# Cross attentions: projections one per three steps, output projection and division in steps of their own, norms over four steps

## The chip, the cores and the metric

The kernel runs on one core of one Trainium2 chip. A core has TensorE (PE, with its weight loads as PEld), VectorE (DVE), ScalarE (ACT), GpSimd (POOL) and SyncE (SP), which here issues the transfers. Each engine works through its own list of instructions in order; semaphores tie the lists together. The metric is the device time of one execution in microseconds, lower is better.

## What is computed

Six layers of a decoder, each followed by a residual and a layer norm, on an input of 32 batches x 128 tokens x 128 features. Two of them, `cross0` and `cross1`, are the cross attentions that the change touches; they differ in that the first adds a mask. Cut to what matters:

```python
q = heads(tgt @ Wq + bq) / sqrt(8)        # 16 heads of 8 features
k = heads(memory @ Wk + bk)
v = heads(memory @ Wv + bv)
scores = einsum('bhqd,bhkd->bhqk', q, k)
scores = where(mask[:, None, :, :], NEG_INF, scores)     # first cross attention only
attn = softmax(scores, axis=-1)
ctx = einsum('bhqk,bhkd->bhqd', attn, v).transpose(0, 2, 1, 3).reshape(b, -1, 128)
x = layernorm(x + ctx @ Wo + bo)
```

The other four passes (self attention, two mixtures of experts, attention over positions) are the same in both kernels.

## The kernel before

`cross_attention_pass` holds each cross attention. A batch is a row `r` (32 of them, in 8 quads `q` of four), and a row is split into four units `u` of four heads each, 128 units in all. The loop `for s in steps` runs on every engine over the same step numbers, one unit per step, and `at(s, lag, per, count)` says which item, if any, is due in a step: item `i` comes in step `lag + per * i`. So the lags and the order of the `if` blocks inside a step set each engine's order. A quad is 16 steps, a row four. In what follows a step is odd or even by its number, counted within a row as 0 to 3.

The work of a unit, in the order of the data:

- `scores` (L990; in the masked pass after two mask matmuls, L984): query rows x keys, for two units at a time, in odd steps. VectorE takes the maxima (L1188), POOL splits them into two bf16 parts (L1137, L1139), PE transposes them (`maxT`, L1047) and ScalarE copies them back (L1109).
- `scoresT`: the transposed scores of unit s+2 (L1034, in the masked pass after the mask matmul L1001), interleaved with the subtraction of the maxima of unit s+1 (L1037). Each unit of the 32-row products sits in one of four groups of 32 rows of the array, and the two interleaved ones in different groups, as do the two units of `scores`.
- ScalarE takes the exponential twice, as f16 and as f32 (L1103, L1104), POOL subtracts the one from the other (L1131, `pl`).
- `attended` (L953 to L955 on `avp`): 12 matmuls with 9 columns each, for unit s-2, at the end of the step. It fills one PSUM tile over four steps; VectorE takes the reciprocal (L1176), then a maximum, then the division (`att`, L1194) in the step with number 2 of the row.
- Per row: PE transposes `att` (`attT`, L1058, step 3), ScalarE and VectorE split it (L1113, L1199), PE multiplies with the output weights (L953 to L955 on `msc`, in step 1), VectorE adds the residual (L1225) and takes the statistics (L1232, L1181).
- Per quad: five pieces in `prep` (transposed x, Q, transposed context, K, V), one PSUM tile `prj` for all. Before, one is due every two steps, K twelve and V ten steps ahead of the quad's first unit. SP then lays Q and K out into the four row groups with 12 copies each (L903), loads the next quads (L886, L890, L895) and stores a finished quad (L936). The norm of a quad (L1238, four instructions) stands in one step.

`maxT`, `attT` and the output projection share one PSUM tile, `msc`. `take_misc` makes each wait until the previous user has been read. In the step with number 1 PE runs scoresT, scores, `maxT`, output projection, attended; the output projection waits there for ScalarE's copy of the maxima (`s_mTs`).

## Time and profile before

| | us |
|---|---|
| median of 3 runs | 2220.37 |
| lowest and highest | 2205.09, 2227.87 |
| profiled execution, its own time | 2225.0 |
| its span | 2223.2 |
| PE, DVE, ACT, POOL busy | 1489.2, 1237.8, 793.8, 1011.7 |
| first cross attention, from first to last transfer | 765 to 1174 |
| second cross attention | 1673 to 2000 |

Busy times are sums over passes with different limits, so the page's totals don't say what a step of one pass waits for. For that the stretches of one quad and the lists of waits are read. Weight loads and matmuls overlap, matmul ends are modelled, and a few records of matmuls are missing (of the mask matmul L1001, 66 of 128 are there). PEclk is the share of the full clock that TensorE was granted: 1.0 is 2.4 GHz, 0.5 is 1.2 GHz.

### The profile page before, as it was taken

How to read it: one execution, taken by the hardware profiler on the slowest of the kernel's cores; microseconds unless marked ns; L12 is line 12 of the kernel's file. 1: busy time of each engine (PE TensorE's matmuls, PEld its weight loads, DVE VectorE, ACT ScalarE, POOL GpSimd, SP SyncE). 2: the span in 40 equal slices, each digit the busy share in tenths (PEclk: the TensorE clock that was granted, in tenths of full speed). 3: DMA queues.
4: the chain of work that ended last, by engine and by line, in shares of the span. 5: the costliest groups of instructions: out<-in, count | busy, mean ns of one | idle time of the engine just before them, and what ended most of it. 6: DMA issues, size and time to landing. Idle time of an engine off the chain costs nothing. (4 is left out here: it accounts for less than half of the span.)

```text
span 2223.2 us, 45449 instructions
## 1 busy us (share of the span) xinstructions
PE 1489.2 (67%) x17246; PEld 1022.1 (46%) x17428; DVE 1237.8 (56%) x2931; ACT 793.8 (36%) x1668; POOL 1011.7 (46%) x1132
## 2 busy tenths in 40 slices
PE   4799999999999668888873118890043677753180
PEld 1466656666666434444443107780042455543170
DVE  4688888788896334444436314453462555554354
ACT  2344444444444224444441103330032565541330
POOL 4656455374471225455554650006613566561506
PEclk9999999999999655555655558995585555555595
DMA  2000000000000111111105211222222111104422
GB/s 88 1 9 10 4 10 4 10 9 5 10 4 5 28 39 42 32 33 36 43 6 172 87 46 51 61 65 56 65 71 59 50 37 52 41 19 142 151 70 71
DMA packets 141816, 99.76 MB, mean 45 GB/s; under 512 B 21283, under 2 KB 129101, under 8 KB 141476
## 3 DMA queue, kind: packets, MB, share of 16 engines
q1 hardware_dynamic: 135460, 84.64, 12.8%
q0 software_dynamic: 6144, 12.22, 1.8%
q8 instruction: 143, 2.34, 0.4%
q14 instruction: 69, 0.57, 0.1%
HBM read 50.99 MB, written 33.55 MB: 38 GB/s over the span
## 5 line engine op out<-in xcount | busy, mean ns | idle before, releaser
L1131 POOL TENSOR_TENSOR cross_pl<-cross_pf,cross_ph 128x512 f16<-128x512 f32 x256 | 292.9, 1157 | 156.9 <-ACT cross_pf L1104 137.4
L639 POOL TENSOR_TENSOR own_full<-own_rot 128x512 f32<-128x512 f32 x128 | 162.7, 1271 | 159.3 <-DVE own_rot L714 149.7
L1624 POOL DMA_INDIRECT mix_got<-results,mix_fetch x96 | 95.6, 996 | 284.1 <-DMA results<-mix_yo 256.8
L1188 DVE TENSOR_REDUCE cross_negmax<-cross_scores 128x8 f32<-128x1024 f32 x128 | 152.5, 1191 | 78.0 <-PE cross_scores L990 77.8
L1103 ACT ACTIVATE cross_ph<-cross_scoresT 128x512 f16<-128x512 f32 x256 | 154.9, 605 | 48.1 <-PE cross_scoresT L1037 43.4
L1034 PE MATMUL cross_scoresT<-cross_qt,cross_kt 32*128 32x128 f16 x1024 | 152.0, 299 | 26.2 <-issue 21.8
L631 POOL TENSOR_TENSOR own_qkl<-own_full,own_qkh 128x512 f16<-128x512 f32 x128 | 157.8, 1236 | 0.0
L1104 ACT ACTIVATE cross_pf<-cross_scoresT 128x512 f32<-128x512 f32 x256 | 155.7, 608 | 0.0
L1037 PE MATMUL cross_scoresT<-cross_maxT,cross_sel 32*128 32x128 bf16 x1024 | 152.2, 299 | 0.0
L553 ACT CAST own_qkh<-own_full 128x512 f16<-128x512 f32 x128 | 79.1, 618 | 158.6 <-POOL own_full L639 156.6
L575 ACT ACTIVATE own_ph<-own_scoresT 128x512 f16<-128x512 f32 x128 | 76.5, 598 | 153.1 <-PE own_scoresT L491 153.1
L265 DVE TENSOR_TENSOR own_pl<-own_pf,own_ph 128x512 f16<-128x512 f32 x128 | 127.1, 993 | 1.0 <-ACT own_pf L576 1.0
L953 PE MATMUL cross_attended<-cross_vl,cross_ph 128*128 128x9 f16 x1024 | 114.3, 178 | 19.6 <-DVE cross_att L1194 17.8
L953 PEld LDWEIGHTS cross_attended<-cross_vl,cross_ph 128*128 128x128 f16 x1024 | 103.0, 114 | 46.2 <-DVE cross_att L1194 30.2
L1176 DVE RECIPROCAL cross_recip<-cross_attended 128x16 f32<-128x16 f32 x64 | 16.5, 257 | 186.0 <-PE cross_attended L955 186.0
L1789 DVE SCALAR_TENSOR_TENSOR mix_hl<-mix_pH,mix_hh 128x512 f16<-128x512 f32 x112 | 72.1, 685 | 85.5 <-ACT mix_hh L1569 85.5
L484 PE MATMUL own_scoresT<-own_qkh,own_qkl 64*128 64x128 f16 x512 | 113.6, 222 | 7.3 <-issue 2.1
L1034 PEld LDWEIGHTS cross_scoresT<-cross_qt,cross_kt 32*128 32x128 f16 x1024 | 85.6, 124 | 64.3 <-issue 55.8
L491 PE MATMUL own_scoresT<-own_maxT,own_sel 64*128 64x128 bf16 x512 | 112.7, 220 | 0.0
L486 PE MATMUL own_scoresT<-own_qkh 64*128 64x128 f16 x512 | 112.6, 220 | 0.0
L485 PE MATMUL own_scoresT<-own_qkl,own_qkh 64*128 64x128 f16 x512 | 112.4, 220 | 0.0
L954 PE MATMUL cross_attended<-cross_vh,cross_pl 128*128 128x9 f16 x1024 | 105.0, 169 | 0.0
(332 smaller groups left out, 5451.1 us busy)
## 6 DMA issues: line engine op xcount, KB each, us to landing
mix_stage<-in_mix_w SPq DMA_DIRECT2D x48, 256.0 KB
slots<-mix_blank SPq DMA_DIRECT2D x14, 512.0 KB, 5.9
mix_xg<-slots SPq DMA_DIRECT2D x56, 128.0 KB
results<-mix_yo SPq DMA_DIRECT2D x56, 128.0 KB, 1.8
cross_xin<-after SPq DMA_DIRECT2D x16, 256.0 KB, 2.9
cross_cin<-in_ctx SPq DMA_DIRECT2D x16, 256.0 KB, 3.3
cross_qt<-cross_qnh SPq DMA_DIRECT2D x128, 32.0 KB
cross_kt<-cross_knh SPq DMA_DIRECT2D x128, 32.0 KB
```

The lines of the kernel that those rows point to most:

```text
L265: ops.tensor_tensor(pl[g][:], pf[g % 2][:], ph[g][:], ALU.subtract).then_inc(s_plow, 1)
L484: nc.tensor.matmul(o, kl_, qa, start=False, stop=False, skip_group_check=True)
L491: mm = nc.tensor.matmul(o, sel[r:r + nr, g // 2 if own else g, j, :], maxT[bb % 2][r:r + nr, :], start=False, stop=True, skip_group_check= ...
L631: nc.gpsimd.tensor_tensor(qkl[1 - par][p % 2][:, p // 2, :], full[p % 2][:], qkh[1 - par][p % 2][:, p // 2, :], ALU.subtract)\
L639: nc.gpsimd.tensor_tensor(full[g % 2][:], rot[g % 2][0][:], rot[g % 2][1][:], ALU.add)\
L953: nc.tensor.matmul(out, lh, rl, start=start, stop=False, skip_group_check=True)
L1034: nc.tensor.matmul(out, lhs, rhs, start=first, stop=False, skip_group_check=True)
L1037: mm = nc.tensor.matmul(out, lhs, rhs, start=False, stop=True, skip_group_check=True)
L1103: nc.scalar.activation(ph[u % 4][:], stp[u % 3][:], ACT.Exp, scale=scale)
L1104: nc.scalar.activation(pf[u % 3][:], stp[u % 3][:], ACT.Exp, scale=scale).then_inc(s_exp, 1)
L1131: nc.gpsimd.tensor_tensor(pl[u % 4][:], pf[u % 3][:], ph[u % 4][:], ALU.subtract).then_inc(s_pl, 1)
L1188: nc.vector.tensor_reduce(negmax[rr % 2][:, 2 * a:2 * a + 2, :].rearrange("p u g -> p (u g)"), scp[:].rearrange("p (h t) -> p h t", t=P), ...
```

## The change

Only `cross_attention_pass` changes. The computation and the instructions are the same; their order and their waits are not.

- `prep`: the five pieces of a quad are due at -25, -22, -19, -16, -13 instead of -18, -16, -14, -12, -10. VectorE takes them two steps later instead of one; SP's layouts move to -18 and -14, the loads to -34.
- PE: within a step attended now follows scoresT at once, then `maxT`, `attT`, the scores, the pieces, the output projection. The output projection moves from lag 9 to 10, to the end of step 2.
- ScalarE: the copies of the maxima and of `attT` stand ahead of the exponentials, the pieces behind them.
- VectorE: the division directly follows the reciprocal, ahead of the maximum; residual and statistics come one step later each; the norm's four instructions stand in four different odd steps (27, 29, 31, 33).
- POOL: rstd in step 26 instead of 23. SP: store in step 34 instead of 25.
- `ident4` is loaded with the first constants, so PE, ACT and DVE wait for 48 of `s_const` and 64 of `s_more`.

```diff
-        FIRST, LAST = -18, NU + 26
+        FIRST, LAST = -25, NU + 18
...
-            return [(p, i) for p, lag in ((XT, -18), (Q, -16), (CT, -14), (K, -12), (V, -10))
+            return [(p, i) for p, lag in ((XT, -25), (Q, -22), (CT, -19), (K, -16), (V, -13))
...
-                q = at(s, -15, 16, NQUAD)
+                q = at(s, -18, 16, NQUAD)
                 if q is not None:
                     lay(q, Q, qt, (qnh, qnh, qnl))
-                q = at(s, -11, 16, NQUAD)
+                q = at(s, -14, 16, NQUAD)
                 if q is not None:
                     lay(q, K, kt, (knh, knl, knh))
-                q = at(s, -24, 16, NQUAD)
+                q = at(s, -34, 16, NQUAD)
                 if q:
                     load_x(q)
...
-                r = at(s, 9, UNITS, B)
-                if r is not None:
-                    pe.wait_ge(s_al, r + 1)
-                    take_misc((s_y, r + 1))
-                    three(msc[:, 0:D], attTh[:], attTl[:], wh["o"][:], wl["o"][:], True, True).then_inc(s_o, 1)
...
+                pair = at(s, -7, 2, NU // 2)
+                if pair is not None:
+                    scores(pair)
+                for p, q in prep(s):
+                    project(p, q)
+                r = at(s, 10, UNITS, B)
+                if r is not None:
+                    pe.wait_ge(s_al, r + 1)
+                    take_misc((s_y, r + 1))
+                    three(msc[:, 0:D], attTh[:], attTl[:], wh["o"][:], wl["o"][:], True, True).then_inc(s_o, 1)
...
-                q = at(s, 23, 16, NQUAD)
+                q = at(s, 26, 16, NQUAD)
...
+                    dve.wait_ge(s_rec, r + 1)
+                    late(dve, s_aT, r - 1)
+                    nc.vector.tensor_tensor(att[r % 2][:], v[:, :, 0:DH], recip[:].unsqueeze(2).to_broadcast([P, H, DH]),
+                                            ALU.mult).then_inc(s_att, 1)
...
+                for b in range(QUAD):
+                    q = at(s, 27 + 2 * b, 16, NQUAD)
...
-                for p, q in prep(s - 1):
+                for p, q in prep(s - 2):
```

How the order changes. The first place is PE in the second cross attention, the step in which the maxima are transposed (L990 is the scores, L1047 `maxT`, L953 to L955 on `cross_misc` the output projection, on `cross_attended` attended). Before:

```order
L1034 MATMUL cross_scoresT<-cross_qt,cross_kt 128x128
L1037 MATMUL cross_scoresT<-cross_maxT,cross_sel 128x128
L990 MATMUL cross_scores<-cross_kt,cross_qt 128x128 x8
L1047 MATMUL cross_misc<-cross_ident,cross_max 128x128
L953 MATMUL cross_misc<-cross_wol,cross_attTh 128x128
L954 MATMUL cross_misc<-cross_woh,cross_attTl 128x128
L955 MATMUL cross_misc<-cross_woh,cross_attTh 128x128
L953 MATMUL cross_attended<-cross_vl,cross_ph 128x9
```

The scores directly follow scoresT, and the output projection directly follows `maxT`. The same step after the change (one line further down in the file: L991 is the scores, L1060 `maxT`, L964 a transposed input piece, L1035 and L1038 the next step's scoresT):

```order
L954 MATMUL cross_attended<-cross_vl,cross_ph 128x9
L955 MATMUL cross_attended<-cross_vh,cross_pl 128x9
L956 MATMUL cross_attended<-cross_vh,cross_ph 128x9
L1060 MATMUL cross_misc<-cross_ident,cross_max 128x128
L991 MATMUL cross_scores<-cross_kt,cross_qt 128x128 x8
L964 MATMUL cross_proj<-cross_ident,cross_cin 128x128 x4
L1035 MATMUL cross_scoresT<-cross_qt,cross_kt 128x128
L1038 MATMUL cross_scoresT<-cross_maxT,cross_sel 128x128
```

Attended has moved between scoresT and the scores, and the output projection has left the step: it now ends the next one.

The second place is ScalarE, one row's worth of exponentials up to the copy of the maxima (L1113 copies `attT`, L1109 the maxima). Before:

```order
L1113 CAST cross_attTh<-cross_misc 128x128
L1103 ACTIVATE cross_ph<-cross_scoresT 128x512
L1104 ACTIVATE cross_pf<-cross_scoresT 128x512
L1103 ACTIVATE cross_ph<-cross_scoresT 128x512
L1104 ACTIVATE cross_pf<-cross_scoresT 128x512
L1103 ACTIVATE cross_ph<-cross_scoresT 128x512
L1104 ACTIVATE cross_pf<-cross_scoresT 128x512
L1109 COPY cross_maxT<-cross_misc 128x128
```

And after (L1094 copies `attT`, L1090 the maxima, L1105 takes a piece):

```order
L1094 CAST cross_attTh<-cross_misc 128x128
L1100 ACTIVATE cross_ph<-cross_scoresT 128x512
L1101 ACTIVATE cross_pf<-cross_scoresT 128x512
L1105 CAST cross_xh<-cross_proj 128x512
L1100 ACTIVATE cross_ph<-cross_scoresT 128x512
L1101 ACTIVATE cross_pf<-cross_scoresT 128x512
L1090 COPY cross_maxT<-cross_misc 128x128
L1100 ACTIVATE cross_ph<-cross_scoresT 128x512
```

The copy now stands behind two exponential pairs instead of three.

The third place is the queue of SP in the masked pass, the layouts of one quad (`qt`, `kt`) and the loads of the next. Before:

```order
L903 DMA cross_qt<-cross_qnh 8x4x512 x8
L903 DMA cross_qt<-cross_qnl 8x4x512 x4
L903 DMA cross_kt<-cross_knh 8x4x512 x4
L903 DMA cross_kt<-cross_knl 8x4x512 x4
L903 DMA cross_kt<-cross_knh 8x4x512 x4
L886 DMA cross_xin<-after 128x4x128
L890 DMA cross_cin<-in_ctx 128x4x128
L895 DMA cross_rawmask<-in_mask 128x4x128
```

And after:

```order
L903 DMA cross_qt<-cross_qnh 8x4x512 x8
L903 DMA cross_qt<-cross_qnl 8x4x512 x4
L886 DMA cross_xin<-after 128x4x128
L890 DMA cross_cin<-in_ctx 128x4x128
L895 DMA cross_rawmask<-in_mask 128x4x128
L903 DMA cross_kt<-cross_knh 8x4x512 x4
L903 DMA cross_kt<-cross_knl 8x4x512 x4
L903 DMA cross_kt<-cross_knh 8x4x512 x4
```

The loads have moved from behind K's layout to the place between Q's and K's.

## Rows read from the trace of the kernel before

**Rows 1.** The page's slices: granted clock in tenths, 40 slices of 55.6 us

```profile
PEclk9999999999999655555655558995585555555595
```

**Rows 2.** Busy time in stretches, first cross pass: one quad, then a fast stretch

```profile
core 0: us, PE busy (x) PEld busy (x) DVE busy (x) ACT busy (x) POOL busy (x), PEclk, DMA share, GB/s
...
904.45:950.63 46.18, 40.76 (x455) 22.64 (x462) 19.65 (x41) 21.51 (x46) 23.86 (x28) 0.50 0.13 38
1056.00:1066.00 10.00, 6.78 (x125) 4.27 (x123) 6.60 (x13) 5.33 (x12) 6.84 (x10) 1.00 0.22 66
```

**Rows 3.** Busy time in stretches, same columns: one quad of the second cross pass

```profile
1788.47:1824.05 35.58, 25.91 (x430) 18.57 (x430) 20.21 (x41) 20.61 (x46) 22.19 (x27) 0.50 0.15 46
```

**Rows 4.** Waits 780 to 1180 us: waiting and waited for, us in total, times, longest

```profile
PE cross_scores L984 <- DMA cross_kt<-cross_knh: 17.3, 4, 11.2
...
PE cross_misc L953 <- ACT cross_maxT L1109: 13.7, 29, 1.2
...
PE cross_attended L953 <- DVE cross_att L1194: 7.0, 12, 0.6
```

**Rows 5.** Waits 1690 to 2000 us, the second cross pass

```profile
PE cross_misc L953 <- ACT cross_maxT L1109: 38.9, 29, 1.9
...
PE cross_scores L990 <- DMA cross_kt<-cross_knh: 34.5, 8, 11.8
...
PE cross_attended L953 <- DVE cross_att L1194: 10.8, 10, 1.1
```

**Rows 6.** Timeline of PE: start, duration, engine, line, operation, idle before and releaser

```profile
800.85 1.03 PE L984 MATMUL cross_scores<-cross_addmask,cross_ident 128*128 128x512 bf16 x2 [1.32 <-DVE cross_negmax L1188]
```

**Rows 7.** Timeline of the second cross pass: ScalarE's copy, then PE

```profile
1825.05 0.30 ACT L1109 COPY cross_maxT<-cross_misc 128x128 bf16<-128x128 bf16 x1
1825.49 0.26 PE L953 MATMUL cross_misc<-cross_wol,cross_attTh 128*128 128x128 f16 x1 [1.89 <-ACT cross_maxT L1109]
...
1828.31 0.28 PE L1034 MATMUL cross_scoresT<-cross_qt,cross_kt 32*128 32x128 f16 x1
...
1828.34 0.29 PE L990 MATMUL cross_scores<-cross_kt,cross_qt 32*128 32x128 f16 x2
...
1828.87 0.47 PE L1058 MATMUL cross_misc<-cross_ident,cross_att 128*128 128x128 f32 x1
...
1829.59 0.28 PE L1034 MATMUL cross_scoresT<-cross_qt,cross_kt 32*128 32x128 f16 x1
...
1830.12 0.61 PE L953 MATMUL cross_proj<-cross_cl,cross_wkh 128*128 128x512 f16 x1
```

**Rows 8.** Timeline of PE, first cross pass: masks that begin a step

```profile
840.15 0.59 PE L1001 MATMUL cross_scoresT<-cross_ident,cross_addmask 128*128 128x512 bf16 x1
...
844.75 0.59 PE L1001 MATMUL cross_scoresT<-cross_ident,cross_addmask 128*128 128x512 bf16 x1
...
1104.04 0.38 PE L1001 MATMUL cross_scoresT<-cross_ident,cross_addmask 128*128 128x512 bf16 x1
...
1107.22 0.39 PE L1001 MATMUL cross_scoresT<-cross_ident,cross_addmask 128*128 128x512 bf16 x1
1110.15 0.69 PE L984 MATMUL cross_scores<-cross_addmask,cross_ident 128*128 128x512 bf16 x2 [2.22 <-DMA cross_kt<-cross_knh]
```

**Rows 9.** Timeline of SP's queue: two loads, the last layout group of a quad

```profile
796.32 0.44 SPq L886 DMA_DIRECT2D cross_xin<-after  x1
...
797.36 0.51 SPq L895 DMA_DIRECT2D cross_rawmask<-in_mask  x1
...
1105.67 2.81 SPq L903 DMA_DIRECT2D cross_kt<-cross_knh  x4
```

**Rows 10.** Timeline of DVE and POOL: maximum and second half of the split

```profile
899.87 1.22 DVE L1188 TENSOR_REDUCE cross_negmax<-cross_scores 128x8 f32<-128x1024 f32 x1 [1.07 <-PE cross_scores L990]
...
901.44 0.22 POOL L1139 TENSOR_TENSOR cross_max<-cross_negmax,cross_max 128x16 bf16<-128x16 f32 x1
```

**Rows 11.** Timeline of PE: low-clock scores, K projection before a rise, scores after

```profile
842.18 0.61 PE L990 MATMUL cross_scores<-cross_kt,cross_qt 32*128 32x128 f16 x8
...
1096.96 0.61 PE L953 MATMUL cross_proj<-cross_cl,cross_wkh 128*128 128x512 f16 x1
...
1100.48 0.40 PE L990 MATMUL cross_scores<-cross_kt,cross_qt 32*128 32x128 f16 x8
```

More of the change, by code:

```diff
@@ L908, in _ @@
             sp.dma_start(bias[:], w["bias"]).then_inc(s_const, 16)
+            sp.dma_start(ident4[:], k["ident4"]).then_inc(s_const, 16)
             for n in names[0:2]:
@@ L913, in _ @@
                 sp.dma_start(stage[n][:], w[n]).then_inc(s_w[n], 16)
-            for to, frm in ((ident4[:], k["ident4"]), (sel[:], k["sel"]), (vbias[:], w["vbias"]), (expo[:], k["expo4"]),
+            for to, frm in ((sel[:], k["sel"]), (vbias[:], w["vbias"]), (expo[:], k["expo4"]),
                             (obias[:], w["obias"].partition_broadcast(P))):
@@ L1082, in _ @@
                 nc.scalar.copy(wh[n][:], stage[n][:]).then_inc(s_wh, 1)
-            act.wait_ge(s_const, 32)
+            act.wait_ge(s_const, 48)
             for s in steps:
+                r = at(s, -2, UNITS, B)
+                if r is not None:
+                    act.wait_ge(s_mT, r + 1)
+                    late(act, s_T, UNITS * (r - 1))
+                    nc.scalar.copy(maxT[r % 2][:], msc[:, 0:P // 2].bitcast(BF16)).then_inc(s_mTs, 1)
+                r = at(s, 8, UNITS, B)
+                if r is not None:
+                    act.wait_ge(s_aT, r + 1)
+                    nc.scalar.copy(attTh[:], msc[:, 0:P]).then_inc(s_ah, 1)
+                u = at(s, 0, 1, NU)
+                if u is not None:
+                    act.wait_ge(s_T, u + 1)
+                    late(act, s_av, u - 3)
+                    late(act, s_pl, u - 2)
+                    nc.scalar.activation(ph[u % 4][:], stp[u % 3][:], ACT.Exp, scale=scale)
+                    nc.scalar.activation(pf[u % 3][:], stp[u % 3][:], ACT.Exp, scale=scale).then_inc(s_exp, 1)
                 for p, q in prep(s - 1):
@@ L1166, in _ @@
                 if i == 1:
-                    dve.wait_ge(s_const, 32)
-                    dve.wait_ge(s_more, 16 * 5)
+                    dve.wait_ge(s_const, 48)
+                    dve.wait_ge(s_more, 16 * 4)
                     nc.vector.tensor_copy(vbias_b[:], vbias[:].to_broadcast([P, P])).then_inc(s_vb, 1)
```

122 lines of the change are left out of this document (48 added, 74 removed).

## Prediction

> **What bounds the kernel now.** I read first the slices of the page: the two cross attentions (765 to 1174 us and 1672 to 2000 us) stand in the slices where the granted clock is 5 and not 9 [rows 1]. So TensorE runs there at 1.2 GHz, and the first question is how much of it is work and how much is waiting. A stretch of exactly one quad (16 steps, four batches) tells it. In the first pass a quad takes 46.18 us, with PE busy for 40.76 [rows 2]; the mask matmul of L1001 (0.59 us [rows 8]) is recorded in only about half of the steps, and the eight missing ones, about 0.4 us each beside their neighbours, make PE some 44 us busy. In the second pass a quad takes 35.58 us with PE busy for 25.91, and the next engine, POOL, for 22.19 [rows 3]. The first cross pass is therefore bound by PE at the low clock, the second by waits of PE. The list of waits names them. In the first pass PE waited 13.7 us for ScalarE's copy of the transposed maxima, 7.0 for VectorE's division, and 17.3 for the K transfers, of which 11.2 is one wait at the start [rows 4]. In the second pass the same three are 38.9, 10.8 and 34.5, of which 11.8 at the start [rows 5]. A fourth, 1.32 us for VectorE's maximum, comes twice at the start of each pass [rows 6].
>
> Why the maxima's copy is so late shows in the timeline: ScalarE copies at 1825.05, behind the exponentials of two units, and PE, which asks for the output projection in the same step as that transposition, starts it at 1825.49 after 1.89 us idle [rows 7].
>
> **The change, term by term.** *Output projection one step later, copy ahead of the exponentials.* Between the transposition and the output projection now lie the scores (odd step) and the next step's scoresT and attended; the copy is ScalarE's first work of its step. The wait goes: 13.7 + 38.9 us. Cover if I am wrong: 0.45 us per row (32 rows a pass), the smallest value now.
>
> *Attended ahead of the scores, division straight after the reciprocal.* Before, the division stands behind a 1.2 us maximum while PE is already at the next row's attended. Now attended ends ahead of `maxT` and the scores, earlier by their length, and nothing stands between reciprocal and division: 7.0 + 10.8 us go.
>
> *Projections earlier.* K is projected nine steps before its first scores instead of five. The queue then needs 24 copies of 0.70 us (groups of four in 2.81 us) and two or three loads of 0.5 between Q and K [rows 9]; the last copy landed about 1.7 us after its issue, if the start of the scores at 1110.15 is set against the last group's start at 1105.67 [rows 8, 9]. That is 16.9 + 1.5 + 1.7 = 20 us, counted from the scoresT that frees the Q buffer, eleven steps ahead of the scores. A second-pass quad of work alone is 25.9 us busy now [rows 3] and 8 x 0.5 us for the scores (below), 29.9 in all; eleven steps of it are 20.6, and the place in the step adds 1. So the wait goes, by a small margin in the second pass and a wide one in the first: 22.7 + 6.1 us. Also the second quad's transposes and Q now fill the ramp, where PE waits for VectorE: 2 x 2 x 1.32 = 5.3 us.
>
> Together 29.4 us in the first pass (13.7 + 7.0 + 6.1 + 2.6) and 75.0 in the second: 104. I take 100, since the last rows of a pass have no later work to cover them.
>
> *What it adds.* The scores lose their company. In the second pass scoresT and the eight scores matmuls now run side by side: from 1828.31 to 1828.87, 0.56 us for both, while a step without scores needs 0.53 (1829.59 to 1830.12) [rows 7]. After the change attended, which uses all rows of the array, stands between them. Eight scores matmuls alone lie between 0 (if they overlap the next scoresT) and their 0.54 us; the next scoresT needs one of the same two row groups, so I take 0.5: 64 x 0.5 = 32 us (0 to 35). In the first pass the mask matmuls separated them already: 0. The Trainium skill, TensorEngine Tiling (Array Packing), Key Properties, says that different tiles of the array load and multiply in parallel and that a change of tiling mode drains the engine. The rows agree with the first half, and it is the rule that speaks against this change; if the scores kept a partner the sum would be 32 us lower.
>
> The loads of the second quad now stand ahead of K in the queue at the start: 796.32 to 797.87 for three [rows 9], so 1.5 and 1.0 us later first scores. Norms in four pieces, earlier rstd, ident4 in another group: the same instructions; VectorE and POOL have 20 and 22 us of work in 35.6 [rows 3], which hides them; uncovered, 0.1 us each.
>
> Sum with the clock as now: 100 - 32 - 2.5 = 65 us. The profiled execution took 2225 us (span 2223.2), 5 more than the median 2220: 2225 - 65 = 2160.
>
> **The clock.** The first pass is not at the low clock throughout. At 1056 to 1066 it was granted 1.00 [rows 2]. The matmuls show it too: between two masks, the same two steps took 4.60 us (840.15 to 844.75) at 1.2 GHz and 3.18 (1104.04 to 1107.22) at 2.4 [rows 8]. Before it rose, PE had run a K projection, scoresT and the scores' masks with one short attended among them (1096.96 on; the scores at 1100.48 take 0.40 us for the eight, at the low clock 0.61) [rows 11]. It fell back each time when PE stood idle for the K transfers, 2.2 us at 1110.15 [rows 8]. The change works on both ends: scores, V projection, mask and scoresT now follow each other with no attended (9 narrow columns per weight load) between, once a quad, and the idle time that ended the fast stretches goes. I expect the rise in the first or second quad and then mostly the high clock: six of eight quads. A quad without waits is 46.2 - 2.4 = 43.8 us at the low clock; times 1.42/4.60 it gains 13.5. Six give 81. The three fast stretches that are in the 2225 already were worth about 7 us, which go off: 2160 + 7 - 81 = **2086 us**. POOL's 23.86 us a quad [rows 2] stays below the 30 that result. The second pass has no masks and so less dense stretches; it stays low.
>
> **Rivals.** *The clock behaves as before* (0.28): the dense stretch doesn't suffice, or, with steps of 1.6 to 1.7 us, K comes late again (20 us against eleven steps of 1.7 = 19) and PE's idle time takes the clock down each quad. For it: only three rises in the whole pass now. 2160, 2140 to 2185.
> *Both passes at the high clock* (0.06). The second pass then falls from 29.9 us a quad toward POOL's 22.2; with the queue's 20 us for eleven steps and POOL's 1.1 to 1.4 for each of five it is about 25.5: 7.5 quads x 4.4 = 33 us less, 2053. Against it: not one fast slice in the second pass now. The Trainium skill, TensorE: Matmul & The Clock Gate, section on why this matters for kernels, advises to avoid idle gaps between bursts to keep the full clock. The trace doesn't agree with that alone: a quad with under 3 us idle in 46 ran at 0.50 [rows 2]; by the page this rival would be the likeliest.
> *The waits move* (0.07): half of the 100 comes back as waits for exponentials or divisions: 2225 - 50 + 34 = 2209, no change.
> *The other side, slower* (0.05): the split of the maxima. The scores are now last in their step, and PE asks for maxT two steps on, after two scoresT and two attended: 0.53 + 0.45 twice = 1.96 us in the second pass. The chain in between is the maximum and two POOL operations, from 899.87 to 901.66, 1.8 us [rows 10]. It fits with 0.15 to spare. If the 1.16 us subtraction on POOL or a norm and a projection piece on VectorE (0.6 + 0.7) come first, PE waits up to 2 us in each of 64 rows: 2160 + 128 = 2288. It decides from 1.0 us per row, which eats the 65. Against it: the subtraction in front belongs to a unit whose exponential ended a step earlier.
>
> **Numbers.** My forecast has 0.54 (own range 2055 to 2130: four to eight fast quads). A difference under 1% (22 us) can't be told from none here. Faster: 0.54 + 0.28 + 0.06 = 0.88; same 0.07; slower 0.05. The range 2045 to 2185 holds the first three cases to their bounds.
>
> **What would show it.** PE's waits for the maxima's copy and the division gone from both passes; a second-pass quad near 29.9 us with PE nearly without idle time; scores alone 0.5 us between transposition and next scoresT; the K wait only at the start; the granted clock above 0.8 over the first pass. A clock of 0.5 there makes it 2160; a wait at the maxT transposition for POOL is the slower case; a clock of 1.0 in the second pass shows that I underrated the density.

## The result and the profile after

| | before | after |
|---|---|---|
| median of 3 runs | 2220.37 | 2093.04 |
| lowest and highest | 2205.09, 2227.87 | 2071.41, 2097.38 |
| profiled execution, its span | 2223.2 | 2091.2 |

The ratio is 0.941, with a 95% interval of 0.928 to 0.954: faster by 5.9%. The two spans differ by 132.0 us. To see where they went, each execution is cut where a pass's first transfer is issued (SP's load at L886 for a cross attention, the mixture's or the position attention's first one behind it). These cuts give the table; "high" is the time within the first cross attention at a granted clock of 1.0, summed from the trace's record of that clock, from its first scores on.

| us | self attention and start | first cross | high | second cross | the three other passes together |
|---|---|---|---|---|---|
| before | 765.2 | 408.8 | 23.9 | 326.7 | 722.5 |
| after | 748.4 | 340.5 | 95.6 | 280.0 | 722.3 |
| difference | -16.8 | -68.3 | | -46.7 | -0.2 |

The page of the changed kernel gives the same picture in two lines: PE's busy tenths, and the granted clock, in slices of 52.3 us. The first cross attention is slices 15 to 21, the second slices 31 to 36.

```profile
PE   4799999999999939999964218891052899953370
...
PEclk9999999999999955569855559996575555555695
```

Where [rows 1] had nothing above 6 in the first cross attention, there are now a 6, a 9 and an 8; the second stays at 5 (slice 31, a 6, begins in the pass before it).

The waits of PE in the first cross attention (748 to 1089 us), then in the second (1587 to 1868 us): waiting and waited for, us in total, times, longest. They answer to [rows 4, 5].

```profile
PE cross_scores L985 <- DMA cross_kt<-cross_knh: 11.4, 3, 7.5
...
PE cross_attended L954 <- POOL cross_pl L1132: 3.0, 5, 0.6
PE cross_misc L1060 <- POOL cross_max L1140: 1.9, 1, 1.9
...
PE cross_scores L991 <- DMA cross_kt<-cross_knh: 13.5, 8, 7.9
...
PE cross_attended L954 <- POOL cross_pl L1132: 3.7, 7, 0.9
PE cross_misc L1060 <- POOL cross_max L1140: 2.1, 2, 1.9
...
PE cross_attended L954 <- DVE cross_att L1180: 1.1, 3, 0.4
```

The wait for ScalarE's copy of the maxima is gone from both lists, the division's from the first and nearly from the second. K's is not only at the start (7.5 and 7.9 us): in the second pass 5.7 us are left in the seven later quads. A stretch of one quad in each pass, in the columns of [rows 2], answers to [rows 2, 3]:

```profile
831.07:874.05 42.98, 42.98 (x463) 21.81 (x464) 19.30 (x39) 21.80 (x46) 23.60 (x29) 0.50 0.11 34
...
1715.45:1744.92 29.47, 28.57 (x435) 19.59 (x434) 20.88 (x42) 21.30 (x47) 22.11 (x28) 0.50 0.18 56
```

The first-pass quad at the low clock takes 43.0 us with PE busy throughout; the second-pass quad takes 29.5 with PE busy for 28.6, where before it was busy for 25.9 of 35.6.

### The profile page after: what moved, and what is told of

Same layout as the page of the kernel before. It is cut to its first block and busy times, and to the rows that moved or that the text cites. A ratio compares the mean times of both kernels' runs of the same rounds, so it can differ in the third digit from the quotient of the medians.

```text
span 2091.2 us, 45631 instructions
## 1 busy us (share of the span) xinstructions
PE 1488.2 (71%) x17428; PEld 1001.5 (48%) x17428; DVE 1248.5 (60%) x2931; ACT 800.6 (38%) x1668; POOL 1008.7 (48%) x1132
## 5 line engine op out<-in xcount | busy, mean ns | idle before, releaser
L1035 PE MATMUL cross_scoresT<-cross_qt,cross_kt 32*128 32x128 f16 x1024 | 143.2, 285 | 0.1
L1038 PE MATMUL cross_scoresT<-cross_maxT,cross_sel 32*128 32x128 bf16 x1024 | 142.4, 281 | 0.0
L1035 PEld LDWEIGHTS cross_scoresT<-cross_qt,cross_kt 32*128 32x128 f16 x1024 | 85.3, 121 | 69.8 <-issue 58.8
L954 PE MATMUL cross_attended<-cross_vl,cross_ph 128*128 128x9 f16 x1024 | 108.7, 173 | 8.1 <-POOL cross_pl L1132 6.7
L954 PEld LDWEIGHTS cross_attended<-cross_vl,cross_ph 128*128 128x128 f16 x1024 | 86.4, 102 | 53.5 <-issue 38.6
L714 DVE SCALAR_TENSOR_TENSOR own_rot<-own_proj,own_bias,own_cos 128x512 f32<-128x512 f32 x128 | 94.9, 742 | 17.2 <-POOL own_full L639 12.8
L956 PE MATMUL cross_attended<-cross_vh,cross_ph 128*128 128x9 f16 x1024 | 104.2, 168 | 0.0
```

The lines of the kernel that those rows point to most:

```text
L954: nc.tensor.matmul(out, lh, rl, start=start, stop=False, skip_group_check=True)
L1035: nc.tensor.matmul(out, lhs, rhs, start=first, stop=False, skip_group_check=True)
L1038: mm = nc.tensor.matmul(out, lhs, rhs, start=False, stop=True, skip_group_check=True)
```

## The experiments

All lengths below are those of the two cross attentions, cut as above, from one profiled execution each. Medians are of whole executions; a ratio is to the kernel before on the same chip and occasion, whose median there lay between 2212.6 and 2224.7. The diffs are cut to their main lines; the recorded text behind each says what else moved.

| kernel | first cross | high | second cross | median | ratio to before, 95% |
|---|---|---|---|---|---|
| before | 408.8 | 23.9 | 326.7 | 2220.4 | |
| 1. before + projections early | 414.8 | 17.1 | 320.2 | 2219.9 | 0.998 (0.994 to 1.002) |
| 2. before + output projection's own step | 383.8 | 51.2 | 316.4 | 2181.2 | 0.983 (0.977 to 0.989) |
| 3. before + attended and division | 399.1 | 51.2 | 327.8 | 2211.2 | 0.994 (0.990 to 0.999) |
| 8. after, old projections | 373.3 | 92.2 | 310.0 | 2172.3 | 0.979 (0.976 to 0.983) |
| after | 340.5 | 95.6 | 280.0 | 2093.0 | 0.941 (0.928 to 0.954) |
| 12. after, once more | 344.6 | 85.3 | 281.2 | 2103.8 | 0.943 (0.937 to 0.949) |
| 11. after, norm in one step | 325.6 | 129.7 | 285.0 | 2109.6 | 0.953 (0.949 to 0.958) |
| 4. after, scores behind scoresT | 321.3 | 160.4 | 276.4 | 2076.8 | 0.936 (0.931 to 0.941) |
| 7. as 4, loads behind K | 343.1 | 150.2 | 294.3 | 2127.0 | 0.957 (0.952 to 0.962) |
| 5. after, three buffers | 312.8 | 146.8 | 276.3 | 2077.8 | 0.937 (0.933 to 0.941) |
| 6. as 4, three buffers | 281.9 | 211.6 | 265.1 | 2038.0 | 0.921 (0.915 to 0.927) |
| 9. as 6, pieces two steps earlier | 282.2 | 218.5 | 263.3 | 2033.8 | 0.917 (0.912 to 0.922) |
| 10. as 9, extra product in second pass | 285.6 | 211.6 | 269.9 | 2036.1 | 0.919 (0.913 to 0.925) |

### One part at a time

**1. Projections early, the rest as before.**

```diff
-            return [(p, i) for p, lag in ((XT, -18), (Q, -16), (CT, -14), (K, -12), (V, -10))
+            return [(p, i) for p, lag in ((XT, -25), (Q, -22), (CT, -19), (K, -16), (V, -13))
...
-                q = at(s, -15, 16, NQUAD)
+                q = at(s, -18, 16, NQUAD)
...
-                q = at(s, -11, 16, NQUAD)
+                q = at(s, -14, 16, NQUAD)
```

> The kernel before with one part of the change: the five pieces of a quad at -25 to -13 (VectorE two steps behind), Q's layout at -18, K's at -14, loads at -34. ScalarE's pieces stand behind its copies, since else two engines would wait for each other. Lengths are from a pass's first transfer to the next pass's; before they are 408.8 us (first cross attention) and 326.7 (second). Theory A, the waits add up as the prediction has them: the K wait from the second quad on goes, 22.7 us in the second pass and 6.1 in the first, and the ramp 2.6 each, less 1.5 and 1.0 for the loads: second pass 303 us, first 402, clock as before. Rival B, the spacing is what lets the clock rise in the first pass: first pass near 340. Rival C, PE waits elsewhere instead (for the exponentials, behind which the pieces no longer stand, or for the maxima's copy): second pass 320 or more.

Median 2219.9, the same as before; first cross attention 414.8 us, second 320.2. Waits of PE in seven quads of the second pass, of the kernel before (1717 to 1966 us), then of this one (1717 to 1965 us):

```profile
PE cross_misc L953 <- ACT cross_maxT L1109: 35.3, 26, 1.9
PE cross_scores L990 <- DMA cross_kt<-cross_knh: 22.7, 7, 6.9
PE cross_attended L953 <- DVE cross_att L1194: 8.7, 8, 1.1
```

```profile
PE cross_misc L954 <- ACT cross_maxT L1097: 32.8, 27, 1.4
PE cross_attended L954 <- DVE cross_att L1195: 30.7, 26, 1.5
PE cross_scores L991 <- DMA cross_kt<-cross_knh: 4.7, 1, 4.7
```

The K wait fell from 22.7 us to 4.7, all of it in one quad, and the division's rose from 8.7 to 30.7. A quad stays at 35.4 us. This is rival C: the time went into another wait. Part of it may lie in ScalarE's pieces, which stand behind the exponentials here; that was not taken apart. The first pass had no more of the high clock than before (17.1 us against 23.9), so the spacing of the projections alone doesn't raise it (rival B falls).

**2. Output projection in its own step, ScalarE's copies ahead of the exponentials.**

```diff
-                r = at(s, 9, UNITS, B)
-                if r is not None:
-                    pe.wait_ge(s_al, r + 1)
...
+                r = at(s, 10, UNITS, B)
+                if r is not None:
+                    pe.wait_ge(s_al, r + 1)
...
             for s in steps:
+                r = at(s, -2, UNITS, B)
+                if r is not None:
+                    act.wait_ge(s_mT, r + 1)
```

> The kernel before with one part: output projection one step later, ScalarE's copies of the maxima and of attT ahead of the exponentials, and what follows on VectorE and POOL moved with it; attended, division and projections as before. Theory A: the wait for the maxima's copy goes, 38.9 us in the second pass and 13.7 in the first; but the K transfers still have only eight to nine steps, and each of them is now 0.3 us shorter in the second pass, so the K wait grows by up to 2.6 us a quad, 18 in all. Second pass 326.7 - 38.9 + 18 = 306 us (288 if K keeps up), first pass 408.8 - 13.7 = 395, clock as before. Rival B: the idle time between steps is what keeps the clock low in the first pass: then it rises here too, first pass 340 to 360. Rival C: the wait moves to attT or the output projection itself: second pass 320 or more.

Median 2181.2; first cross attention 383.8, second 316.4. The wait for the copy is gone, and K's takes much of it back (second pass, 1680 to 1924 us):

```profile
PE cross_scores L990 <- DMA cross_kt<-cross_knh: 36.5, 7, 6.6
PE cross_attended L953 <- DVE cross_att L1194: 18.6, 14, 3.0
```

K 22.7 to 36.5, the division 8.7 to 18.6. Theory A had the direction and K's part (up to 18), but not the division's, so it gave 306. The first pass is 25 us shorter with 27 us more at the high clock: some of rival B, in one profile.

**3. Attended behind scoresT, division behind the reciprocal.**

```diff
+                    dve.wait_ge(s_rec, r + 1)
+                    late(dve, s_aT, r - 1)
+                    nc.vector.tensor_tensor(att[r % 2][:], v[:, :, 0:DH], recip[:].unsqueeze(2).to_broadcast([P, H, DH]),
+                                            ALU.mult).then_inc(s_att, 1)
                 pair = at(s, -6, 2, NU // 2)
```

> The kernel before with one part: attended directly behind scoresT, the division directly behind the reciprocal. Theory A: the division's wait goes (10.8 us second pass, 7.0 first), and the scores lose their company in the second pass: 64 x 0.42 to 0.5 = +27 to 32 us, of which the K wait, which has eight to nine of sixteen steps, takes back about half: second pass 326.7 - 10.8 + 29 - 9 = 336 us; first pass 402 with the clock as before. Rival B: the maxima's copy comes less late since PE asks for it later in the step, so second pass 326 or less. Rival C: the order without attended between scores, V, mask and scoresT is what raises the clock in the first pass: first pass 340 to 370.

Median 2211.2; first cross attention 399.1, second 327.8. Neither 336 nor below 326: the waits left in the second pass (1700 to 1950 us) are

```profile
PE cross_misc L953 <- ACT cross_maxT L1109: 21.4, 26, 1.3
PE cross_scores L990 <- DMA cross_kt<-cross_knh: 13.4, 7, 4.9
```

so the maxima's copy fell from 35.3 to 21.4 us, which theory A left out, and K's from 22.7 to 13.4, as it had it; PE's extra work filled the rest. The first pass came out near theory A's 402, and not at rival C's 340 to 370: its clock rises in five quads, each time behind a K projection and the next mask, and each time for 10.2 us only, up to a K wait of some 1.7 us.

**8. The changed kernel with the old projections.**

```diff
-            return [(p, i) for p, lag in ((XT, -25), (Q, -22), (CT, -19), (K, -16), (V, -13))
+            return [(p, i) for p, lag in ((XT, -18), (Q, -16), (CT, -14), (K, -12), (V, -10))
```

> The changed kernel with the pieces, layouts and loads at their old lags (-18, -16, -14, -12, -10; -15, -11; -24), all else changed. It tells whether the parts add up. Theory A, they don't: each wait covers the next, and with K projected nine steps... that is five steps ahead of its scores the K chain sets the quad at about 34.8 us whatever PE saves elsewhere, as it did where only the output projection was moved: second pass 312 to 318 us, K waits of 35 or more. Rival B, the parts add up, so only the early K's 22.7 us are missing: 303 us. First pass at the low clock: K has time there, so 384 to 400 us, and if the early projections are not needed for the clock to rise, 340 to 360.

Second cross attention 310.0 us, a little below theory A's range (a quad of 33.3 to 34.3), with the K waits that it gave (1680 to 1917 us):

```profile
PE cross_scores L991 <- DMA cross_kt<-cross_knh: 37.1, 7, 6.5
```

The first took 373.3 us, between both ranges given for it, with 92.2 us at the high clock. So the early projections aren't needed for the clock to rise. In the second pass the three parts alone are worth 6.5, 10.3 and -1.1 us, 15.7 together; all at once 46.7, of which some 5 are the norm's (kernel 11), which none of the three has. Early projections alone brought 6.5 us, as the last part 30.0. **The parts don't add up: the waits of one quad lie over each other**, and as long as K takes some twenty microseconds from a late start, whatever PE saves elsewhere it spends waiting there.

### What bounds the second cross attention now

**4. Scores directly behind scoresT again.**

```diff
                 if u1 is not None:
                     mm.then_inc(s_T, 1)
+                pair = at(s, -7, 2, NU // 2)
+                if pair is not None:
+                    scores(pair)
...
-                pair = at(s, -7, 2, NU // 2)
-                if pair is not None:
-                    scores(pair)
```

> The changed kernel with one part undone: the scores directly behind scoresT again, attended behind them. Changed kernel: 340.5 us in the first cross attention, 280.0 in the second. Theory A: the overlap comes back in the second pass, 64 x 0.42 = 27 us less work, but eleven steps are then 18 us against a K chain of 19 to 20, so 1 to 2 us a quad of K wait come back: 263 us (253 to 266). In the first pass the scores follow scoresT and attended stands ahead of V projection and mask again: if the row without attended is what raised the clock, the pass goes back to 390 us; rival B, it was the missing idle time, the pass stays at 330 to 350. Rival C, attended, now last ahead of the maxima's transposition, is late for VectorE's division, which costs 0.5 us a row: second pass 275 or more.

**5. Three buffers for the laid-out Q and K.**

```diff
-        qt, kt = many(2, "qt", [P, HU, WIDTH], F16), many(2, "kt", [P, HU, WIDTH], F16)
+        qt, kt = many(3, "qt", [P, HU, WIDTH], F16), many(3, "kt", [P, HU, WIDTH], F16)
...
-                late(sp, s_T, 4 * UNITS * (q - 1))
+                late(sp, s_T, 4 * UNITS * (q - 2))
```

> The changed kernel with three buffers for the laid-out Q and K instead of two (zeroed by two more memsets), Q's layout asked for at -20. The queue then needn't wait for the previous quad's last scoresT. Changed kernel: 340.5 and 280.0 us, PE busy 28.6 us of a second-pass quad of 29.2. Theory A: with the scores last in their step the second pass is bound by PE itself, since the scores lost their company: only the 5.7 us of K waits go, 274 us. Rival B, the K chain is what sets the 29.2 us quad and PE's busy time is stretched to it: 262 us or less. First pass: the K waits of the fast quads go, 3.9 us, and if it is the idle time at K that takes the clock down, the fast stretches become longer: 340 - 4 to 340 - 20 us.

**6. Both edits, 4's and 5's, together** (the two diffs above).

> The changed kernel with the scores directly behind scoresT and with three buffers for Q and K: the previous run's edit and the one of the scores together. With the scores first and two buffers the second pass took 276.4 us, with 21.6 us of K waits in seven quads, PE busy 25.9 us of a quad of 29.1. Theory A: the K chain was the bound there, and the overlap of the scores was worth 27 us but hidden behind it: second pass 276.4 - 21.6 = 255 us, a quad of 26.2. Rival B: PE waits for exponentials or for POOL instead (POOL is busy 22.4 us of a quad): 265 us or more. First pass: 321.3 us with two buffers, of which 10.3 is K waits from the second quad on: 311 us if the clock stays as it is, 295 to 305 if these waits are what takes it down.

The second pass took 276.4 us with kernel 4, 276.3 with 5 and 265.1 with 6. One quad of each, 4, 5 and 6 in turn, in the columns of [rows 2]:

```profile
1662.12:1691.81 29.69, 25.66 (x435) 17.42 (x434) 20.50 (x42) 20.89 (x46) 22.26 (x28) 0.50 0.19 55
```

```profile
1685.60:1714.30 28.70, 28.51 (x436) 19.59 (x433) 21.42 (x43) 21.20 (x46) 22.13 (x28) 0.50 0.20 58
```

```profile
1658.58:1685.95 27.37, 25.39 (x423) 17.13 (x421) 20.49 (x43) 20.59 (x45) 22.22 (x28) 0.50 0.20 61
```

These are two limits of nearly the same size. With the scores last PE is busy for 28.5 us of 28.7 (kernel 5): PE is the bound, and the scores' lost company is 28.57 - 25.66 = 2.9 us a quad, 0.36 for each of eight scores. With the scores first (kernel 4) PE needs only 25.7, but its quads take 29.0 to 29.7, because K is late; its waits in seven quads (1604 to 1808 us) are

```profile
PE cross_scores L991 <- DMA cross_kt<-cross_knh: 21.6, 7, 4.5
PE cross_scoresT L1035 <- ACT cross_pf L1101: 3.9, 10, 0.4
```

Either edit alone is worth 4 us in the second pass, both together 15: again more than their sum. For kernel 4 rival C's length came (276.4 against "275 or more"), but not by its cause, the division, which costs 0.2 us there: theory A had the cause, and undersized the K wait (3.1 us a quad, not 1 to 2). Kernel 6 missed its 255 by 10 us: the K wait is still 10.2 us in seven quads, since with the third buffer Q's layout starts as soon as the low half of Q is there, which in turn is late (SP waited 56.1 us for it in those quads). The first passes took 312.8 us (expected 320 to 336) and 281.9 (295 to 311), with 146.8 and 211.6 us at the high clock. For kernel 4 I had expected 390 us there if the row without attended counts, since attended now stood ahead of the V projection; it came out at 321.3, 9 us below rival B's 330 to 350; the section on the clock comes back to it.

**7. As kernel 4, with the loads behind K's layout.**

```diff
-                q = at(s, -34, 16, NQUAD)
+                q = at(s, -29, 16, NQUAD)
```

> The changed kernel with the scores directly behind scoresT, two buffers, and the next quads' loads asked for behind K's layout (-29) instead of between Q's and K's (-34). Theory A: if a second-pass quad is the K chain (24 copies of 0.70, the landing, and the two loads between) plus the six steps outside it, then it gets 1.0 us shorter by the two loads: 276.4 - 7.5 x 1.0 = 269 us, and in the first pass 1.5 us a quad at the high clock: 321 - 10 = 311. Rival B, the loads cost the queue nothing because the copies wait for something else (their data): 276 as before.

A miss: 294.3 us instead of 269. The wait moved from K to the next quad's input (second pass, 1657 to 1882 us):

```profile
PE cross_proj L964 <- DMA cross_xin<-after: 38.3, 6, 7.4
...
PE cross_scores L991 <- DMA cross_kt<-cross_knh: 2.1, 1, 2.1
```

The expectation counted the queue's time and not who waits for the loads: they stand behind copies which wait for the buffer, and PE asks for the input a few steps later. Placing the loads between Q and K, which the prediction booked as a small cost, is what keeps them in time.

**9. As kernel 6, the pieces two steps earlier.**

```diff
-            return [(p, i) for p, lag in ((XT, -25), (Q, -22), (CT, -19), (K, -16), (V, -13))
+            return [(p, i) for p, lag in ((XT, -27), (Q, -24), (CT, -21), (K, -18), (V, -14))
```

> Scores first and three buffers, as in the run that took 281.9 and 265.1 us, and the pieces two steps earlier (-27, -24, -21, -18, -14; layouts at -22 and -16, loads at -36). There the second pass still waited 10.2 us in seven quads for the K transfers, since its chain now starts at the low half of Q. Theory A: two steps are 3.3 us more than the 1.5 us a quad that is missing, so the second pass goes to 255 us (a quad of 26.2, PE busy 25.7), the first stays at 282. Rival B: another engine comes next (the exponentials, 4.3 us there), so 260 or more. Rival C: V, one step earlier, waits for the previous quad's attended and holds ScalarE: both passes longer than there.

Median 2033.8, 0.917 of the time before, against 0.941 and 0.943 for the changed kernel; kernels 6 and 10 (0.921, 0.919) can't be told from it. Second pass 263.3 us, so rival B: K is in time in all quads but two, and the next waits take its place (1576 to 1776 us):

```profile
PE cross_attended L956 <- DVE cross_att L1184: 6.4, 6, 1.2
PE cross_scores L993 <- DMA cross_kt<-cross_knh: 6.3, 2, 4.6
PE cross_scoresT L1037 <- ACT cross_pf L1103: 6.3, 15, 0.8
```

**11. The changed kernel with the norm in one step.**

```diff
-                for b in range(QUAD):
-                    q = at(s, 27 + 2 * b, 16, NQUAD)
+                q = at(s, 27, 16, NQUAD)
```

> The changed kernel with one part undone: the norm's four instructions in one step again (27), the store where it is. Theory A, spreading them costs and gains nothing, since VectorE has work for 21 of 29 us in a second-pass quad: second pass 280 +- 1 us. Rival B: four in a row, 2 us, hold the maxima, so PE waits for the maxima or for their split in one row a quad: up to 1.5 x 8 = 12 us more, second pass 285 to 292. The first pass varies with the clock and tells nothing here below 15 us.

Second pass 285.0 against 280.0 and 281.2: rival B, at the lower edge of its range. The wait at the maxima's transposition is what grew, from 2.1 us to

```profile
PE cross_misc L1060 <- POOL cross_max L1140: 7.3, 6, 1.9
```

So the spreading, for which the prediction took nothing, is worth 4 to 5 us in this pass: it keeps the chain maximum, split, transposition free.

### The clock in the first cross attention

**12. The changed kernel once more.**

> The changed kernel once more, word for word, on another occasion, to tell what of its gain repeats. The second pass runs at the low clock throughout, so its length should repeat within 1 us: 280. The first pass hangs on when the clock rises; the kernel with its norm in one step, which can only be slower, took 325.6 us there against 340.5 in the changed kernel's profile, so theory A: the moment of the rise is chance, and the pass comes out anywhere from 320 to 350 us. Theory B: it follows from the order of the instructions, so 340 +- 2, and the norm's edit was worth 15 us by itself. The self attention, untouched, took 748 to 774 us in the profiles so far; it should fall in there again. Median 2080 to 2100 us.

Theory A for the moment of the rise: it came at 886.1 us in an execution whose pass began at 749.5, in the third quad instead of the fourth. Quads of 32.3, 32.2, 34.7 and 40.2 us followed. In all, 344.6 us with 85.3 at the high clock, and the second pass 281.2. The median came out at 2103.8, above the 2080 to 2100 expected. The self attention, the same code in all kernels, took between 748.4 and 774.1 us in the fourteen profiles; the 765.2 and 748.4 of before and after are two draws from that.

What PE ran before the rise in the changed kernel (timeline; scoresT, one attended and `maxT` between 909.99 and 911.68 are left out):

```profile
908.44 0.59 PE L954 MATMUL cross_proj<-cross_xl,cross_wqh 128*128 128x512 f16 x1
908.82 0.63 PE L955 MATMUL cross_proj<-cross_xh,cross_wql 128*128 128x512 f16 x1
909.24 0.63 PE L956 MATMUL cross_proj<-cross_xh,cross_wqh 128*128 128x512 f16 x1
909.67 0.31 PE L954 MATMUL cross_misc<-cross_wol,cross_attTh 128*128 128x128 f16 x1
...
909.99 0.63 PE L1002 MATMUL cross_scoresT<-cross_ident,cross_addmask 128*128 128x512 bf16 x1
...
911.68 0.85 PE L985 MATMUL cross_scores<-cross_addmask,cross_ident 128*128 128x512 bf16 x2
912.47 0.40 PE L991 MATMUL cross_scores<-cross_kt,cross_qt 32*128 32x128 f16 x8
```

The scores at 912.47 take 0.40 us, at the low clock 0.61 [rows 11]. The first long fast stretches of kernels 4, 5, 6, 9, 11 and 12 began within 5 us behind such a place too: three products of a Q or K projection, the next step's mask, scoresT, the two masks of the scores. Before the change attended, 12 matmuls of 9 columns, stood between a projection and the next mask; in the changed kernel and in 5, 11 and 12 it stands behind scoresT, and in 4, 6 and 9, where the scores directly follow scoresT, not even one attended lies in the row.

How much of this the clock answers to is open. In 4, 6 and 9 it first rises 38 to 51 us into the pass and in 12 and after 137 to 164, but in kernels 8 and 11, with attended where the changed kernel has it, 50 and 77 us in. In the changed kernel four such rows, behind the projections at 822.4, 838.8, 865.4 and 881.9, passed without a rise. Kernel 2 was 51 us at the high clock with attended in its old place. And the place needn't be a Q or K projection: kernel 10's first pass, 211.6 us at the high clock, rose at 803.8 behind a V projection (its last product, the next mask, the masks of the scores):

```profile
801.82 0.31 PE L958 MATMUL cross_proj<-cross_wvh,cross_ch 128*128 128x128 f16 x1
801.92 0.63 PE L1004 MATMUL cross_scoresT<-cross_ident,cross_addmask 128*128 128x512 bf16 x1
...
803.03 0.99 PE L987 MATMUL cross_scores<-cross_addmask,cross_ident 128*128 128x512 bf16 x2
803.95 0.40 PE L993 MATMUL cross_scores<-cross_kt,cross_qt 32*128 32x128 f16 x8
```

Which products raise the clock was not isolated in this pass. Kernel 10 tries it in the other.

**10. One wide product more per step in the second pass**, in kernel 9.

```diff
+                else:
+                    nc.tensor.matmul(stp[u % 3][:], ident4[:, 0:P], ident4[:], start=True, stop=False,
+                                     skip_group_check=True)
```

> The previous kernel with one product more in each step of the second pass, of the form and at the place of the mask product of L1001 (128 rows, 512 columns, bf16); its result is overwritten, so the computation stays as it is. It asks what keeps the second pass at the low clock. Theory A, it is the lack of wide products: with the extra one the granted clock rises there too, and a quad takes 25 to 26 us, as the first pass's 28.3 at the high clock less its eight mask pairs of the scores (3.4 us): second pass 250 to 260 us. Theory B, something else (the waits, or what ran before the pass): the clock stays at 0.5, and each product costs its 0.38 to 0.43 us: 16 x 0.4 = 6.4 us a quad, second pass 305 to 310 us.

Theory A for the clock, half of it for the time. In stretches of the second pass (columns of [rows 2]) the granted clock is

```profile
1600.00:1640.00 40.00, 36.77 (x618) 22.30 (x612) 27.19 (x53) 28.08 (x61) 29.46 (x35) 0.71 0.19 58
1640.00:1680.00 40.00, 35.43 (x690) 21.78 (x688) 31.08 (x62) 32.97 (x73) 33.96 (x42) 0.91 0.19 56
1680.00:1720.00 40.00, 35.32 (x621) 21.32 (x620) 30.99 (x62) 29.09 (x64) 31.97 (x40) 0.77 0.22 66
```

where it was 0.50 in every kernel without that product: 99.0 us at the high clock in the pass, where the others have none. The pass takes 269.9 us, against 263.3 without and, by the expectation's estimate, 305 or more if the clock had stayed. PE's busy share alone doesn't do it: kernel 5 had PE busy for 28.51 of 28.70 us there, at 0.50. So it is wide products that the second pass lacks for the high clock, and buying them this way costs more than the clock gives back.

What takes the clock down shows in kernels 4, 5 and 6. Kernel 5's fast stretch of 71.7 us ended at 913.6, and PE's idle times in the 10 us ahead of that are

```profile
906.85 0.17 PE L956 MATMUL cross_attended<-cross_vl,cross_ph 128*128 128x9 f16 x1 [0.65 <-POOL cross_pl L1136]
...
912.52 0.60 PE L987 MATMUL cross_scores<-cross_addmask,cross_ident 128*128 128x512 bf16 x2 [0.62 <-DMA cross_kt<-cross_knh]
```

and for the next 48 us PE was busy without a gap at 0.50 (a stretch of them, then a quad of kernel 6 at the high clock):

```profile
915.00:955.00 40.00, 40.00 (x432) 20.62 (x431) 19.29 (x39) 20.14 (x42) 22.18 (x26) 0.50 0.15 43
```

```profile
860.13:888.46 28.33, 27.34 (x464) 15.77 (x462) 20.60 (x43) 20.49 (x45) 23.84 (x29) 1.00 0.21 61
```

Kernel 4, with 10.3 us of K waits in the first pass (six, of 0.7 to 2.4 us), has five stretches of 27 to 38 us and one of 14, and each of the six ends in a K wait or within 2.1 us behind one. Kernel 6, the same with the third buffer and no K wait after the start, has one of 17 and then one of 194.6 us, up to the last quad. So idle time of PE ends the high clock, and its absence doesn't bring it back. How much it takes is open: kernel 5's stretch outlasted three idle times of 0.64 and 0.65 us (the first one above and two before it, 28 us apart), and the changed kernel's clock fell behind single ones of 0.64, as well as at K waits of 2.95 and 0.92 us.

## Why the prediction was right or wrong

The forecast of 2086 us lies 7 us below the median; its sum was right in total and wrong in its terms. That they evened out is luck, part of it in a pass that the change doesn't touch.

**The waits that go (100 us): right.** Both waits for ScalarE's copy and, but for 1.1 us, the division's are gone; the place of the output projection and of the copy was the cause, as kernel 2 shows. That they could be summed was true only because all three were removed together: one at a time they bring 6.5, 10.3 and -1.1 us of 46.7 in the second pass.

**K's margin: too optimistic.** The step "eleven steps of it are 20.6" against a chain of 20 left a small margin in the second pass and a wide one in the first. In fact there was none: 5.7 us of K waits remain in the second pass, and in the first pass one of 2.95 us at 970.54, in a fast quad. The rival "K comes late again at high clock" had it right, though it was not the likeliest.

**The scores' company (32 us): direction right, size 23.** PE's busy time is higher by 28.6 - 25.7 = 2.9 us a quad (after against kernel 4), 0.36 us instead of 0.5 for each scores. The timeline of the changed kernel shows why: the scores run partly beside the next step's subtraction, which begins 0.09 us after them.

```profile
1686.93 0.39 PE L991 MATMUL cross_scores<-cross_kt,cross_qt 32*128 32x128 f16 x4
1687.02 0.28 PE L1038 MATMUL cross_scoresT<-cross_maxT,cross_sel 32*128 32x128 bf16 x1
...
1687.34 0.31 PE L1035 MATMUL cross_scoresT<-cross_qt,cross_kt 32*128 32x128 f16 x1
```

The forecast quad of 29.9 came out at 29.1 to 30.4, and the pass at -46.7 us against 75 - 32 - 1 = -42. The rule of the Trainium skill's page TensorEngine Tiling (Array Packing), Key Properties, that different tiles work in parallel, agrees with these rows once more. It was weighed as worth 32 us to keep the partner; keeping it alone (kernel 4) brought 4, because the K chain was as long as PE's work.

**The clock (81 us, less 7): mis-sized by half.** Right were the two levels of a quad: 43.0 us at the low clock (43.8 forecast), and 28.3 at the high one in kernel 6, whose scores stand elsewhere, 14.7 less (13.5 forecast). Wrong was the number of fast quads, "the rise in the first or second quad": it came in the fourth, and with four falls behind it there are 95.6 us at the high clock instead of some 180. Two falls are at K waits, as the rival "K comes late again" had it; two are behind waits of 0.64 us for POOL's `pl`, which the prediction didn't have. By these 14.7 us of gain in 28.3 us, 0.52 a microsecond, the 95.6 us are worth 50 and the 23.9 before 12, so some 37 us instead of 74 (an estimate; the prediction took 7 for the 23.9). The first pass's other 31 us are its waits and ramp, forecast as 29 - 1.5. Its place in the code, "scores, V projection, mask and scoresT", is not shown either: the changed kernel's four rises stand behind a Q projection, kernel 10's in the first pass behind V's. Of the mechanism, two parts are shown, that wide products raise the clock (kernel 10, in the second pass) and that idle time takes it down (kernel 6 against 4). That it takes a row without attended is not: kernels 2 and 3 have 51 us at the high clock with attended in theirs. The Trainium skill, TensorE: Matmul & The Clock Gate, section on why this matters for kernels, has TensorE kept busy to get the full clock and gaps avoided to keep it. The rows agree for the fall (kernel 6 against 4), though shorter idle times than the page warns of sufficed (0.64 us), and not for the rise (kernel 5 at 0.50 with PE busy for 40.00 of 40 us).

**What made up for it.** 37 us less from the clock; 5 more in the second pass, 3 more of waits in the first, the 4 of 104 that I had left out for the end of the passes, and 16.8 from the self attention, the same code in both (65.5 + 74 = 139.5 forecast between the two profiles; 139.5 - 37 + 5 + 3 + 4 + 17 = 132): its length varies by 26 us over the profiles. The prediction had no term for that scatter. In the changed kernel's second profile it was as short (749.5), so it can't be averaged out of these two either; against the mean of the fourteen, 758.8, the profile of after is 10 us short and that of before 6 long.

**Norms in four pieces, taken as nothing: wrong by 4 to 5 us**, a gain. The cover was there on the average, VectorE's 21 us of 29, but not at the place: four instructions in a row stand ahead of a maximum whose chain had 0.15 us of slack by the prediction's own sum. The slower rival named exactly this chain; in the changed kernel it holds, with 2.1 us of waits, as long as nothing long is put in front.

## What to carry to other kernels

Waits of one engine that sit in the same period can lie over each other: remove one alone and the next fills its place (6.5 us of 46.7 here), so a part is judged with the others in, and "it brought nothing alone" is no reason to drop it. Two limits of equal size, here PE at 28.6 us and the K chain at 29 us a quad, hide each other in the same way: the third buffer and the scores' order brought 4 us each and 15 together. Where a chain of transfers has to fit in a fixed number of steps, work out its margin at the shortest step that the change can lead to.

## What was not expected of the hardware

- The high clock hardly shortens narrow work. Mean times in kernel 6, first pass at 1.00 (830 to 1020 us), then second at 0.50 (1600 to 1760 us):

```profile
L956 PE MATMUL cross_attended<-cross_vl,cross_ph 128*128 128x9 f16 x432 | 43.9, 170 | 1.9 <-POOL cross_pl L1136 1.0
...
L1037 PE MATMUL cross_scoresT<-cross_qt,cross_kt 32*128 32x128 f16 x429 | 42.2, 217 | 0.0
```

```profile
L1037 PE MATMUL cross_scoresT<-cross_qt,cross_kt 32*128 32x128 f16 x380 | 57.0, 301 | 3.4 <-ACT cross_pf L1103 2.8
L956 PE MATMUL cross_attended<-cross_vl,cross_ph 128*128 128x9 f16 x376 | 40.5, 174 | 0.4 <-DVE cross_att L1184 0.2
```

  Attended's 9 columns take 170 ns and 174 ns, scoresT's 128 columns 217 and 301 (ends of matmuls are modelled, but attended's also start 0.03 us apart at both levels). It fits that twice the clock makes a quad of the first pass 1.5 times as fast, 43.0 and 28.3 us, and not twice.
- The high clock ended 1.1 us behind the second of two idle times, 0.65 and 0.62 us, 5.7 us apart, after single ones of 0.65 had left it up (kernel 5), and lasted 194.6 us with PE's idle time at 1.0 of 28.3 us in a quad (kernel 6). What it takes to bring it back while PE is busy is left open.
- The same kernel's rise came in the fourth quad in one profile and in the third in the other, with the same order of instructions.
